# A fused block of linear attention and gated FFN: the down product as one level of Strassen, its weight combinations streamed from DRAM

## The chip, the cores and the metric

The kernel runs on one core of one Trainium2 chip. The metric is the device time of one execution in microseconds. TensorE (PE) multiplies; VectorE (DVE), ScalarE (ACT) and GpSimd (POOL) do the rest; SyncE (SP) issues nearly all DMAs. Each engine works through an order of its own and waits on semaphores.

## What is computed

u has shape (2, 2048, 512), all in float32. Cut to what matters here:

```python
xn = layernorm(u)                            # over 512
z, x, B, C, dt = split(xn @ in_proj_w)       # 1024, 1024, 64, 64, 16
x = silu(causal_conv1d(x))                   # 4 taps
y = ssd(elu(C)+1, elu(B)+1, x, decay(dt))    # 16 heads of 64, state 64
y = rmsnorm(y + D*x) * silu(z)
attn = y @ out_proj_w                        # 1024 -> 512
g = fwht(xn * SU_ug) / 64                    # Hadamard transform over 512
h = silu(g @ W_gate.T * s_g) * (g @ W_up.T * s_u)    # 2048
ffn = (fwht(h * SU_dp) / 64) @ W_down.T * s_d        # 2048 -> 512
out = u + attn + ffn
```

## The kernel before

A prologue folds the Hadamard transforms and scales into the weights and splits each weight into two float16 parts, high and low. Each product of float32 matrices is then three matmuls (high x high, high x low, low x high; `three`, line 915). All weights stay in SBUF; the down weights are `wd` (line 164), 16 chunks of 128 x 512, both parts.

Then 16 blocks of 256 rows follow (8 for each sequence, carrying a state). What each engine does in a block is written out by hand in the lists `PE_STEPS`, `ACT_STEPS`, `DVE_STEPS`, `POOL_STEPS` and `SP_STEPS` (lines 55 to 77). A name is a step with its index, and every step of a list waits for what it reads and for the buffer it writes. The steps that matter here:
- `bc`, `xp`, `z`: projections of xn from `xnT` (xn turned, in float16 parts). `elu`, `cv`, `tl`, `kl`, `dec`, `ml`, `int`, `itr`, `st`, `vl`, `sl`: the attention part. `ssq`: the root of the norm of y. `ln*`, `xh`, `xl`: layernorm and split of the next block's x.
- `F0` to `F15`: on PE, gate and up of one chunk of 128 of the 2048, 24 matmuls of 256 columns (line 936); on ACT the silu (line 1059); on DVE the product with up, into `tg` (line 1236). `H` (ACT) makes its float16 high part, `L` (DVE, line 1240) the low part, in `h`, three buffers.
- `D0` to `D15` (PE, line 943): the down product of one chunk, 2 tiles of rows x 3 matmuls of 512 columns, summed in two PSUM banks `acc`.
- `O0`, `O1` (PE, line 1003): the output product of the attention for one tile of 128 rows, added in the same banks, 24 matmuls of 512 columns each.
- `fin` (DVE, `final_sum`, line 1335): scales `acc` and adds it to the residual `res`, two operations, one block late: it stands behind `bc` of the next block.
- On SP `td` turns v, `yd` turns the gated y (two DMA transposes for each half) and `xd` turns the next x into `xnT` (four DMA transposes, `turn_x`, line 261), `res` loads the residual, `store` stores the block before. `yd11` waits for `yl11` of DVE. `xd` stands behind `yd11` in the one queue of SP, and waits itself for F15 and z11, the last readers of `xnT`. `bc` of the next block waits for all four transposes (line 923).

PSUM has 8 banks: four form a ring for all steps of `RING_READER` (line 104), each step taking the bank that the fourth step before it had; two alternate for F; two are `acc`.

The order around `bc` at a block's start is `bc xp0 xp1 F0 qk cs F1` on PE and `bc fin elu cv0 cv1 F0` on DVE.

## Time and profile before

| | |
|---|---|
| median of 3 runs | 1849.04 us (1848.91 to 1849.53) |
| profiled execution | 1849.29 us, span 1847.2 us, mean granted TensorE clock 0.996 |
| PE busy | 1794.1 us, 13746 matmuls |
| DVE busy | 1383.8 us |
| ACT busy | 1224.6 us |
| POOL busy | 307.7 us |
| DMA | 125.68 MB, mean 68 GB/s |

Line numbers (L912) are those of the kernel before; L912 is the one line that issues all matmuls of `three` and `products`. Times are in us from the start of the span. In a view in order of time the columns are start, duration, engine, line, operation, output<-input, shapes and number of instructions, and in square brackets how long the engine stood idle before it and for what. A duration reaches to the end of the last result, so it is longer than the distance to the next start. Engines that stand idle cost nothing by themselves: what counts is which wait ends last.

### The profile page before, as it was taken

The page shows a single profiled execution, that of the slowest core. Times are in us where ns is not written, and L with a number is a line of the kernel's source. Part 1 is how long each engine was busy: PE and PEld are TensorE (multiplying, and loading weights), DVE is VectorE, ACT ScalarE, POOL GpSimd, SP SyncE. Part 2 cuts the span into 40 slices and gives each one's busy share as a digit, 9 for nine tenths or more (in the row PEclk, how much of TensorE's full clock was granted, in tenths as well). Part 3 has the DMA queues.
Part 4 walks back from the last instruction along what each step waited for, and adds up shares of the span by engine and source line. Part 5 has one row for each costly group of instructions (what it writes and reads, how often), then busy time and mean ns, then how long its engine had stood idle before and what let it go on. Part 6 is the DMA issues. An engine that isn't in the chain of part 4 may idle for free.

```text
span 1847.2 us, 37874 instructions
## 1 busy us (share of the span) xinstructions
PE 1794.1 (97%) x13746; PEld 1241.8 (67%) x13746; DVE 1383.8 (75%) x2859; ACT 1224.6 (66%) x2582; POOL 307.7 (17%) x270
## 2 busy tenths in 40 slices
PE   4878999999999999999999999999999999999998
PEld 2336667576766768676766758677666757676675
DVE  6987867869586877858586877958686776958686
ACT  7967848576574848566584847666584857667483
POOL 0000212213030212203021221203021220303021
PEclk9999999999999999999999999999999999999999
DMA  8221223121312223131312322131322213131232
GB/s 326 69 69 49 56 58 81 32 82 38 81 47 62 77 47 76 41 78 41 89 47 58 81 45 76 36 77 47 86 53 58 81 34 75 43 81 47 65 75 58
DMA packets 217573, 125.68 MB, mean 68 GB/s; under 512 B 179662, under 2 KB 180790, under 8 KB 216886
## 3 DMA queue, kind: packets, MB, share of 16 engines
q1 hardware_dynamic: 216870, 122.30, 25.1%
q8 instruction: 109, 1.79, 0.4%
q10 hardware_dynamic: 528, 1.05, 0.2%
q14 instruction: 66, 0.54, 0.1%
HBM read 72.18 MB, written 8.65 MB: 44 GB/s over the span
## 4 chain that ended last, share of the span: by engine, by line
PE 90%; DVE 5%; ACT 1%; DMA 1%; issue 1%; SPq 1%; DVEq 1%; ACTq 0%
PE bank L912 88%; DVE wug L624 1%; DVE wi L666 1%; DMA wi<-n_L_attn_out_proj_w_dram 1%; PE bank L728 1%; PE bank L729 0%; DVE big L509 0%; ACT big L460 0%; DVE wo L675 0%; ACT wi L432 0%; SPq L873 0%; PE bank L717 0%; DVE wd L509 0%; DVE big L510 0%; ACT wi L464 0%
## 5 line engine op out<-in xcount | busy, mean ns | idle before, releaser
L912 PE MATMUL bank<-pair,wug 128*128 128x256 f16 x6144 | 699.8, 273 | 0.0
L912 PEld LDWEIGHTS bank<-pair,wug 128*128 128x128 f16 x6144 | 596.2, 98 | 90.4 <-issue 3.4
L912 PE MATMUL bank<-wd,h 128*128 128x512 f16 x1536 | 360.3, 379 | 0.0
L1185 POOL TENSOR_TENSOR state<-state,dec 128x512 f32<-128x512 f32 x64 | 87.5, 1377 | 1066.3 <-ACT neg L1100 805.7
L912 PEld LDWEIGHTS bank<-wd,h 128*128 128x128 f16 x1536 | 149.2, 98 | 160.4 <-DVE h L1243 0.2
L1232 DVE SCALAR_TENSOR_TENSOR pair<-pair,conv 128x256 f32<-128x256 f32 x384 | 180.2, 514 | 79.0 <-ACT pair L1048 69.1
L912 PE MATMUL bank<-wi,pair 128*128 128x512 f16 (+1 forms) x1152 | 201.6, 330 | 3.1 <-DVEq L1345 3.1
L912 PE MATMUL bank<-pair,wi 128*128 128x256 f16 x1536 | 173.1, 273 | 0.0
L912 PEld LDWEIGHTS bank<-wi,pair 128*128 128x128 f16 x1152 | 101.4, 99 | 98.1 <-issue 3.9
L1114 ACT ACTIVATE Mx<-Mx,cs_own 128x128 f32<-128x128 f32 x512 | 162.2, 388 | 7.6 <-DMA Mx<-cs_rows 7.4
L912 PEld LDWEIGHTS bank<-pair,wi 128*128 128x128 f16 x1536 | 150.0, 98 | 17.0
L1173 POOL TENSOR_TENSOR pair<-v 128x512 f32<-128x512 f16 x64 | 79.5, 1242 | 429.4 <-DMA v<-pair 381.4
L1265 DVE TENSOR_TENSOR Mx<-Mx,Gm 128x512 f32<-128x512 f32 x128 | 99.6, 778 | 32.3 <-ACT Mx L1118 22.5
L1063 ACT ACTIVATE pair<-bank,gate_scale 128x256 f32<-128x256 f32 x128 | 60.4, 472 | 92.1 <-PE bank L912 68.2
L1092 ACT ACTIVATE stateK<-state 128x512 f16<-128x512 f32 x64 | 39.7, 620 | 90.0 <-DVE state L1297 90.0
L1297 DVE SCALAR_TENSOR_TENSOR state<-bank,state 128x512 f32<-128x512 f32 x64 | 44.0, 687 | 72.6 <-PE bank L912 72.2
L1063 ACT ACTIVATE tg<-bank,gate_scale 128x256 f32<-128x256 f32 x128 | 59.9, 468 | 49.7 <-PE bank L912 48.8
L1239 DVE SCALAR_TENSOR_TENSOR tg<-tg,h_scale,bank 128x256 f32<-128x256 f32 x128 | 60.9, 476 | 37.8 <-ACT tg L1063 34.2
L1270 DVE TENSOR_TENSOR Mx<-Mx 128x512 f16<-128x512 f32 x96 | 77.2, 804 | 12.7 <-ACT Mx L1129 10.6
L1118 ACT ACTIVATE Mx<-Mx 128x512 f32<-128x512 f32 x128 | 80.6, 630 | 8.1
L912 PE MATMUL bank<-wo,yT 128*128 128x512 f16 x384 | 85.5, 379 | 0.0
L912 PE MATMUL bank<-wo,Mx 128*128 128x512 f16 x384 | 85.5, 379 | 0.0
(253 smaller groups left out, 2717.0 us busy)
## 6 DMA issues: line engine op xcount, KB each, us to landing
Mx<-cs_rows SPq DMA_DIRECT2D x128, 256.0 KB, 3.6
pair<-in_L_attn_u_dram SPq DMA_DIRECT2D x17, 512.0 KB, 3.6
Mx<-in_L_attn_u_dram SPq DMA_DIRECT2D x16, 512.0 KB, 3.7
out_dram<-Mx SPq DMA_DIRECT2D x16, 512.0 KB, 2.8
big<-in_L_ffn_W_down_dram SPq DMA_DIRECT2D x2, 2048.0 KB, 17.8
wug<-in_L_attn_in_proj_w_dram SPq DMA_DIRECT2D x2, 2048.0 KB, 13.4
pair<-in_L_ffn_W_gate_dram SPq DMA_DIRECT2D x4, 1024.0 KB, 5.3
pair<-in_L_ffn_W_up_dram SPq DMA_DIRECT2D x3, 1024.0 KB, 16.6
```

The lines of the kernel that those rows point to most:

```text
L912: ins = nc.tensor.matmul(out, lhsT, rhs, start=first and n == 0, stop=last and n == len(pairs) - 1)
L1063: nc.scalar.activation(tg[c % 2][:, :], ug[c % 2][:, 0:TB], ACT.Silu, scale=gate_scale[:, c:c + 1]).then_inc(gate_ready, 1)
L1092: nc.scalar.activation(stateK[:, hf * 512:(hf + 1) * 512], state[:, hf * 512:(hf + 1) * 512], ACT.Copy, scale=1.0 / LOW).then_inc(state_hi ...
L1114: nc.scalar.activation(M[q][:, n, :], M[q][:, n, :], ACT.Relu, scale=-1.0, bias=cs_own[:, c, 4 * q + n:4 * q + n + 1])
L1118: nc.scalar.activation(M[q][:, :, :], M[q][:, :, :], ACT.Exp, scale=-1.0).then_inc(M_exp, 1)
L1173: pool.tensor_tensor(by_tile(vd[:, :]), v16[:, 4 * hf:4 * hf + 4, c, 0, :], v16[:, 4 * hf:4 * hf + 4, c, 1, :], ALU.add)
L1185: pool.tensor_tensor(half, half, bcast(dec3[:, 2, c, 8 * hf:8 * hf + 8], HD), ALU.mult).then_inc(state_faded, 1)
L1232: ins = nc.vector.scalar_tensor_tensor(cv[n % 2][:, c, :], x[:, c, j:j + TB], conv[:, CX * j + t:CX * j + t + 1], cv[n % 2][:, c, :], ALU. ...
L1239: nc.vector.scalar_tensor_tensor(tg[c % 2][:, :], tg[c % 2][:, :], h_scale[:, c:c + 1], ug[c % 2][:, TB:2 * TB], ALU.mult, ALU.mult).then_ ...
L1265: nc.vector.tensor_tensor(M[q][:, :, :], M[q][:, :, :], Gm[:, c, :].unsqueeze(1).to_broadcast([P, 4, P]), ALU.mult).then_inc(M_whole, 1)
L1270: nc.vector.tensor_tensor(M_lo[q], M[q][:, :, :], M_hi[q], ALU.subtract).then_inc(M_ready, 1)
L1297: nc.vector.scalar_tensor_tensor(half, o[:, :], 1.0 / PEAK, half, ALU.mult, ALU.add).then_inc(dve_emptied, 1)
```

## The change

The down product of a block is a (256 x 2048) by (2048 x 512) product. The change takes it in 8 groups of 256 of the 2048 (`E0` to `E7`, two F chunks each), and each group as one level of Strassen: a matrix of 2 x 2 tiles of 128 x 128 (rows by depth) times one of 2 x 2 tiles of 128 x 256 gives seven products in place of eight. Each is three matmuls of 256 columns, summed over the groups in seven half banks of PSUM, `acc`, now four banks.
- The left sides: `S` on DVE (`half_sums`) forms five sums of the four tiles of h in three operations, with a drain ahead; `H` and `L` split seven tiles of 128 in place of two halves of 256.
- The right sides: the prologue forms five sums of each group's weight tiles on DVE (`ds`, `part_sums`, the same three operations), splits the seven on ACT (`dh`) and DVE (`dl`) in place of the 16 H steps of `wd` on DVE, and SP stores them in DRAM (`dw`). `wd` is gone. In each block ACT loads them back, 896 KB a group, into three buffers `ws` (`wl0` to `wl7`).
- `fin` adds the seven products to four quarters of `res`: six operations with drains. It moves behind `cv0`. `O0` and `O1` take a ring bank each, and DVE adds them to `res` (`out_part`), ahead of `bc` of the next block.
- F takes its bank from the ring of four, which so serves 42 steps a block; `tg` has four buffers.
- All five orders are new, those of the prologue too. The small loads of the prologue move from SP to ACT, and SP loads `nat0` and `nat1` (weights of up) first. PE starts block 0 without waiting for the whole prologue. SP's and POOL's loops over the blocks are unrolled.

The core of the diff:

```diff
 PE_STEPS = """
-bc xp0 xp1 F0 qk cs F1 xp2 xp3 F2 F3 F4 G F5 D0 D1 D2 int00 int01 F6 F7 D3 D4 D5 itr00 F8 F9 itr01 D6 st00 F10
-D7 F11 st01 D8 z00 int10 z01 D9 itr10 F12 F13 int11 D10 itr11 st10 F14 D11 z10 z11 F15 D12 O0 D13 D14 st11 D15
-O1
+bc xp0 xp1 cs xp2 qk F0 F1 F2 F3 G xp3 F4 F5 F6 int00 E0 F7 F8 E1 F9 itr00 st00 E2 int01 F10 itr01 F11 st01
+z00 F12 int10 E3 z01 E4 F13 F14 itr10 int11 st10 F15 E5 itr11 z10 z11 O0 E6 E7 st11 O1
 """.split()
 ACT_STEPS = """
-elu xp0 xb0 xp1 qk xb1 cs F0 sv0 kh sv1 th0 F1 th1 xp2 H0 H1 xp3 F2 dr00 F3 xb2 dr01 xb3 dr02 sv2 H2 th2 H3
-sv3 F4 th3 F5 de00 de01 de02 H4 H5 mh00 dr03 mh01 de03 F6 F7 mh02 H6 vh00 H7 mh03 F8 dr10 F9 de10 H8 H9 vh01
-dr11 mh10 de11 sh00 dr12 ssq0 dr13 mh11 de12 de13 F10 F11 mh12 z00 vh10 H10 H11 sh01 mh13 F12 z01 F13 yh00
-yh01 vh11 ssq1 xh0 z10 H12 H13 xh1 F14 yh10 z11 sh10 H14 yh11 F15 H15 sh11
+elu wl0 xp0 xb0 xp1 cs sv0 xb1 qk F0 th0 xp2 kh dr00 F1 sv1 th1 F2 H0 F3 xb2 dr01 xp3 xb3 wl1 sv2 dr02 th2 F4
+sv3 wl2 F5 th3 de00 H1 de01 de02 mh00 dr03 mh01 de03 F6 wl3 vh00 F7 H2 F8 mh02 H3 F9 mh03 wl4 vh01 dr10 sh00
+de10 F10 H4 ssq0 mh10 F11 dr11 z00 F12 dr12 sh01 de11 de12 vh10 wl5 dr13 de13 H5 z01 F13 mh11 mh12 F14 wl6
+yh00 mh13 wl7 yh01 vh11 F15 H6 ssq1 sh10 xh0 z10 yh10 z11 H7 yh11 xh1 sh11
 """.split()
 DVE_STEPS = """
-bc fin elu cv0 cv1 F0 kl tl0 F1 tl1 L0 L1 qk F2 F3 cv2 cv3 L2 G tl2 L3 F4 tl3 F5 dec00 dec01 dec02 L4 ml00 L5
-ml01 dec03 F6 F7 ml02 int00 L6 vl00 ml03 L7 F8 lna F9 itr00 dec10 int01 st00 L8 itr01 vl01 ml10 L9 sl00 dec11
-st01 ssq0 ml11 dec12 dec13 F10 F11 int10 ml12 L10 z00 L11 vl10 sl01 ml13 F12 itr10 lnb int11 z01 yl00 itr11
-F13 yl01 lnc vl11 ssq1 L12 z10 L13 st10 F14 yl10 z11 L14 xl0 yl11 F15 xl1 L15 st11 sl10 sl11
+O0 O1 bc elu cv0 fin cv1 qk tl0 kl F0 F1 tl1 S0 G F2 L0 F3 cv2 cv3 F4 tl2 S1 tl3 F5 dec00 L1 dec01 ml00 dec02
+S2 dec03 ml01 F6 int00 vl00 F7 L2 S3 F8 itr00 ml02 F9 ml03 st00 L3 vl01 S4 int01 dec10 F10 itr01 sl00 L4 st01
+lna F11 ssq0 z00 S5 lnb dec11 ml10 dec12 F12 vl10 dec13 int10 sl01 L5 ml11 lnc F13 F14 itr10 ml12 yl00 z01 S6
+ml13 int11 yl01 st10 itr11 vl11 L6 F15 S7 ssq1 z10 yl10 z11 xl0 sl10 yl11 L7 xl1 st11 sl11
 """.split()
 POOL_STEPS = """
-sd00 sd01 vw00 vw01 sd10 vw10 sd11 vw11
+sd00 vw00 vw01 sd01 vw10 vw11 sd10 sd11
 """.split()
 SP_STEPS = """
-store bw bd00 bd01 bd02 bd03 td0 td1 td2 td3 xin bd10 bd11 bd12 bd13 yd00 yd01 yd10 yd11 xd res
+bw bd00 store td0 bd01 td1 bd02 bd03 td2 td3 bd10 bd11 xin bd12 bd13 yd00 yd01 yd10 yd11 res xd
...
 
+            def part_sums(eng, ops, n):
+
+                b, o = part[n % 2], part_sum[n % 2]
+                eng.wait_ge(hw_high, UG_UNITS + 2 * n + 2)
+                if n >= 2:
+                    eng.wait_ge(part_ready, n - 1)
+                ops.tensor_tensor(o[:, 0:2, :], b[:, 0::2, :], b[:, 1::2, :], ALU.add)
+                ops.tensor_tensor(o[:, 2:4, :], b[:, 2:4, :], b[:, 0:2, :], ALU.subtract)
+                ops.tensor_tensor(o[:, 4, :], b[:, 0, :], b[:, 3, :], ALU.add).then_inc(part_summed, 1)
+
...
+                    elif k == "dh":
+                        act.drain()
+                        act.wait_ge(part_summed, n + 1)
+                        if n >= 2:
+                            act.wait_ge(wd_stored[n % 2], 16 * (n // 2))
+                        nc.scalar.activation(part_out[n % 2][:, 0:2, 0, :], part[n % 2][:, 0::3, :], ACT.Copy)
+                        nc.scalar.activation(part_out[n % 2][:, 2:7, 0, :], part_sum[n % 2], ACT.Copy).then_inc(part_high, 1)
...
+                    elif k == "ds":
+                        part_sums(dve, nc.vector, n)
+                    elif k == "dl":
+                        dve.wait_ge(part_high, n + 1)
+                        o = part_out[n % 2]
+                        nc.vector.tensor_tensor(o[:, 0:2, 1, :], part[n % 2][:, 0::3, :], o[:, 0:2, 0, :], ALU.subtract)
+                        nc.vector.tensor_tensor(o[:, 2:7, 1, :], part_sum[n % 2], o[:, 2:7, 0, :], ALU.subtract).then_inc(part_ready, 1)
...
             def bank(i, s):
 
                 prior, ago = before(s)
+                if kind(prior) == "F":
+                    pe.wait_ge(h_whole, (i + 1 - ago) * KF + index_of(prior) + 1)
+                    return position(s)
...
                     elif k == "F":
                         c = number(at)
-                        pe.wait_ge(h_whole, (i + 1) * KF + c - 1)
+                        o = bank(i, s)
                         for n, col in enumerate((FF + c * P, c * P)):
-                            ins = products(ug[c % 2][:, n * TB:(n + 1) * TB],
+                            ins = products(o[:, n * TB:(n + 1) * TB],
...
-                    elif k == "D":
-                        c = number(at)
-                        pe.wait_ge(h_ready, (i + 1) * KF + c + 1)
-                        if c == 0:
+                    elif k == "E":
+                        n = at[0]
+                        g = i * KG + n
+                        pe.wait_ge(h_ready, g + KG + 1)
+                        pe.wait_ge(wd_loaded[g % 3], (g // 3 + 1) * 16)
+                        if n == 0:
                             pe.wait_ge(acc_emptied, i + 1)
-                        for j in range(NT):
-                            ins = products(acc[j][:, :], three(lambda u: h[c % 3][:, u, j * P:(j + 1) * P], lambda u: wd[:, c, u, :]),
-                                           first=c == 0, last=c == KF - 1 and down_closes(j))
+                        a, w = hs[g % 2], ws[g % 3]
+                        for left, right, to in ((5, 3, M7), (2, 1, M5), (3, 0, M2), (4, 2, M6), (6, 6, M1), (1, 4, M4), (0, 5, M3)):
+                            ins = products(acc[:, to, :], three(lambda u: a[:, u, left, :], lambda u: w[:, right, u, :]),
+                                           first=n == 0 and to in (M7, M2, M1, M3), last=n == KG - 1)
                         ins.then_inc(h_used, 1)
...
-                        products(acc[c][:, :], [pq for a in range(CX) for pq in three(lambda u: yT[c][:, a, u, :], lambda u: wo[:, a, u, :])],
-                                 first=False, last=not down_closes(c)).then_inc(acc_filled, 1)
+                        o = bank(i, s)
+                        products(o[:, :], [pq for a in range(CX) for pq in three(lambda u: yT[c][:, a, u, :], lambda u: wo[:, a, u, :])]).then_inc(ring_filled, 1)
...
+                    elif k == "wl":
+                        g = i * KG + at[0]
+                        if i == 0:
...
+                        act.wait_ge(h_used, g + KG - 2)
+                        act.dma_start(ws[g % 3][:, :, :, :], wd_dram[at[0]]).then_inc(wd_loaded[g % 3], 16)
                     elif k == "H":
...
+                        n = at[0]
+                        act.wait_ge(h_used, (i + 1) * KG + n - 1)
+                        act.wait_ge(summed, (i + 1) * KG + n + 1)
+                        nc.scalar.activation(hs[n % 2][:, 0, 0:2, :], tp[n % 2][:, 0::3, :], ACT.Copy)
+                        nc.scalar.activation(hs[n % 2][:, 0, 2:7, :], hsum[:, :, :], ACT.Copy).then_inc(h_high, 1)
...
+        def half_sums(eng, ops, i, n):
+
+            x = tp[n % 2]
...
+            eng.wait_ge(h_whole, (i + 1) * KF + 2 * n + 2)
+            eng.wait_ge(h_ready, (i + 1) * KG + n)
+            ops.tensor_tensor(hsum[:, 0:2, :], x[:, 0:2, :], x[:, 2:4, :], ALU.add)
+            ops.tensor_tensor(hsum[:, 2:4, :], x[:, 1:3, :], x[:, 0::3, :], ALU.subtract)
+            ops.tensor_tensor(hsum[:, 4, :], x[:, 0, :], x[:, 3, :], ALU.add).then_inc(summed, 1)
...
+                    elif k == "S":
+                        dve.drain()
+                        half_sums(dve, nc.vector, i, at[0])
...
+                        n = at[0]
+                        dve.wait_ge(h_high, (i + 1) * KG + n + 1)
+                        nc.vector.tensor_tensor(hs[n % 2][:, 1, 0:2, :], tp[n % 2][:, 0::3, :], hs[n % 2][:, 0, 0:2, :], ALU.subtract)
+                        nc.vector.tensor_tensor(hs[n % 2][:, 1, 2:7, :], hsum[:, :, :], hs[n % 2][:, 0, 2:7, :], ALU.subtract).then_inc(h_ready, 1)
...
+            def out_part(i, j):
+                dve.wait_ge(res_loaded, i * 16)
+                dve.wait_ge(ring_filled, i * NR + filled(f"O{j}"))
+                nc.vector.scalar_tensor_tensor(res[:, j, :], position(f"O{j}")[:, :], S_OUT, res[:, j, :], ALU.mult, ALU.add).then_inc(dve_emptied, 1)
...
+                dve.wait_ge(h_used, (i + 1) * KG)
+                quarter = res[:, :, :].rearrange("p j (s n) -> p (j s) n", s=2)
+                both = lambda m: acc[:, m, :].unsqueeze(1).to_broadcast([P, 2, HALF])
+                for terms, to, scale in ((acc[:, M7:M5 + 1, :], quarter[:, 0:2, :], S_OUT), (acc[:, M2:M6 + 1, :], quarter[:, 2:4, :], S_OUT),
+                                         (both(M1), quarter[:, 0::3, :], S_OUT), (both(M3), quarter[:, 1::2, :], S_NEG),
+                                         (both(M4), quarter[:, 0::2, :], S_OUT), (acc[:, M5:M2 + 1, :], quarter[:, 0::3, :], S_NEG)):
+                    dve.drain()
+                    ins = nc.vector.scalar_tensor_tensor(to, terms, scale, to, ALU.mult, ALU.add)
+                ins.then_inc(out_ready, NT)
                 dve.wait_ge(out_ready, i * NT)
                 dve.sem_inc(acc_emptied, 1)
```

## Rows read from the trace of the kernel before

**Rows 1.** The page, part 1: busy us, share of the span.
```profile
PE 1794.1 (97%) x13746; PEld 1241.8 (67%) x13746; DVE 1383.8 (75%) x2859; ACT 1224.6 (66%) x2582; POOL 307.7 (17%) x270
```

**Rows 2.** Windows of one block: us, busy by engine, clock, DMA share, GB/s.
```profile
791.30:896.20 104.90, 104.90 (x836) 73.82 (x835) 78.25 (x162) 68.84 (x147) 18.86 (x16) 1.00 0.23 61
```

**Rows 3.** TensorE in order of time: start, us, line, operation, number.
```profile
811.86 8.02 PE L912 MATMUL bank<-pair,wug 128*128 128x256 f16 x72
819.81 0.23 PE L912 MATMUL bank<-qK,kT 64*128 64x128 f16 x1
822.88 4.05 PE L912 MATMUL bank<-wd,h 128*128 128x512 f16 x18
826.76 0.38 PE L912 MATMUL bank<-stateK,qK 128*128 128x512 f16 x1
```

**Rows 4.** VectorE in order of time, mid-block, back to back.
```profile
838.04 0.68 DVE L1279 TENSOR_TENSOR pair<-bank,dec 128x512 f32<-128x512 f32 x1
838.79 0.75 DVE L1283 SCALAR_TENSOR_TENSOR pair<-pair,scal 128x512 f32<-128x512 f32 x1
839.46 0.42 DVE L1243 TENSOR_TENSOR h<-pair,h 128x256 f16<-128x256 f32 x1
839.80 0.68 DVE L1301 TENSOR_TENSOR vw<-vw 128x512 f16<-128x512 f32 x1
840.40 0.69 DVE L1270 TENSOR_TENSOR Mx<-Mx 128x512 f16<-128x512 f32 x1
841.00 1.38 DVE L1243 TENSOR_TENSOR h<-tg,h 128x256 f16<-128x256 f32 x1
```

**Rows 5.** VectorE: first operation of bc, last of yl11.
```profile
794.44 0.48 DVE L1203 TENSOR_SCALAR raw<-bank,scal 128x256 f32<-128x256 f32 x1 [5.90 <-PE bank L912]
...
885.47 0.68 DVE L1322 TENSOR_TENSOR neg<-v,Gm 128x512 f16<-128x512 f32 x1
```

**Rows 6.** Waits of VectorE, 794.44 to 885.3: total, times, longest; first and last.
```profile
DVE raw L1203 <- PE bank L912: 5.9, 1, 5.9
...
DVE kq L1214 <- DVE Mx L1340: 0.2, 1, 0.2
```

**Rows 7.** SP's queue and TensorE ahead of a block: yd11, x, res; bc.
```profile
886.66 1.20 SPq L873 DMA_TRANSPOSE Mx<-Gm  x1
...
893.58 1.27 SPq L266 DMA_TRANSPOSE pair<-pair  x1
895.12 0.41 SPq L857 DMA_DIRECT2D Mx<-in_L_attn_u_dram  x1
...
897.63 1.66 PE L912 MATMUL bank<-wi,pair 128*128 128x144 f16 x24
```

**Rows 8.** VectorE at the start of block 0, where no fin stands.
```profile
166.82 0.43 DVE L1214 SCALAR_TENSOR_TENSOR kq<-raw,neg 128x256 f32<-128x256 f32 x1 [0.57 <-ACT neg L1053]
...
168.41 0.19 DVE L1218 SCALAR_TENSOR_TENSOR pair<-raw,pair 128x32 f32<-128x32 f32 x1 [0.96 <-ACT pair L1055]
...
170.26 2.79 DVE L1232 SCALAR_TENSOR_TENSOR pair<-pair,conv 128x256 f32<-128x256 f32 x6 [1.14 <-ACT pair L1048]
```

**Rows 9.** TensorE at the start of block 0: windows; bc in time order.
```profile
161.80:164.00 2.20, 2.13 (x19) 2.16 (x20) 1.59 (x4) 0.00 (x0) 0.00 (x0) 0.50 0.03 7
...
161.87 3.04 PE L912 MATMUL bank<-wi,pair 128*128 128x144 f16 x24 [3.08 <-DVEq L1345]
```

**Rows 10.** GpSimd in order of time.
```profile
840.65 1.45 POOL L1173 TENSOR_TENSOR pair<-v 128x512 f32<-128x512 f16 x1 [3.08 <-DVE vw L1301]
```

**Rows 11.** VectorE at the end of the last block.
```profile
1842.49 1.41 DVE L1340 SCALAR_TENSOR_TENSOR Mx<-bank,scal,Mx 128x512 f32<-128x512 f32 x2 [4.99 <-DMA Mx<-in_L_attn_u_dram]
```

**Rows 12.** DMA issues (KB each, us to landing); waits of VectorE ahead of 161.87.
```profile
pair<-in_L_attn_u_dram SPq DMA_DIRECT2D x17, 512.0 KB, 3.6
...
pair<-pair SPq DMA_TRANSPOSE x68, 2.5
...
DVE wo L509 <- DMA pair<-in_L_ffn_W_up_dram: 14.4, 2, 13.3
```

## What the change will do to the time

> **What bounds the kernel now.** I read the page's busy shares first: the matmuls are busy for 97% of the span [rows 1]. Then I cut the span into stretches. The prologue ends where bc of block 0 starts, at 161.87 us [rows 9]; 16 blocks of 104.9 us each follow. In one of them TensorE is busy for 104.90 of 104.90 us, VectorE for 78 and ScalarE for 69 [rows 2]. So a block lasts as long as its matmuls, and VectorE has 26 us left. The question is whether these 26 us are free time. The next views (VectorE in order of time, its waits, the transposes on SP's queue) say that they are not all free.
>
> **What the change gives TensorE.** Eighteen D matmuls of 512 columns take 3.88 us from start to start (822.88 to 826.76), 0.2156 each; 72 F matmuls of 256 columns take 7.95 us (811.86 to 819.81), 0.1104 each [rows 3]. A block has 16 D steps of 6 matmuls: 96 x 0.2156 = 20.70 us. It gets 8 E steps of 7 products x 3 matmuls of 256 columns: 168 x 0.1104 = 18.55 us. Each E matmul loads its own stationary, as each F matmul does, so F's price holds. The gain is 2.15 us a block, 34 us in 16, and a block can't be shorter than 102.75 us.
>
> **What it gives VectorE.** From start to start [rows 4]: a two-tensor operation of 256 elements takes 0.34 us (839.46 to 839.80), one of 512 takes 0.60 (839.80 to 840.40), so I put 640 at 0.74 and 128 at 0.21; a scalar_tensor_tensor of 512 takes 0.67 (838.79 to 839.46), so one of 256 about 0.4. A drain between two costs some 0.15 more (838.04 to 838.79 is 0.75 where 0.60 would do).
> - S, new, 8 a block: 0.34 + 0.34 + 0.21, and 0.14 for its drain. 8.2 us.
> - L: 16 x 0.34 = 5.4 us become 8 x (0.34 + 0.74) = 8.6. 3.2 us more.
> - fin: 1.41 us for two operations (the last block shows it alone [rows 11]) become six with drains, 6 x 0.81 = 4.9. 3.5 us more.
> - O0 and O1 now pass through VectorE: 2 x 0.67 = 1.3 us.
> Together 16.2 us a block, on 78 busy us plus the 5 us of small gaps that no wait accounts for: 99 of the 102.75 that TensorE would need. That alone would just fit.
>
> **Why it doesn't fit.** The next block's bc can't start before xnT is turned. SP issues these four transposes behind yd11, and yd11 waits for yl11 on VectorE. VectorE must then wait for bc before it goes on. So there is a ring: bc filled, VectorE's work up to yl11, yd11, xd, bc. Its length after the change, term by term:
> - VectorE from bc (794.44) to the end of yl11 (885.47 + 0.68 = 886.15) takes 91.7 us now [rows 5]. Twelve waits are listed in it, from 5.9 us down to 0.2 [rows 6]. The 5.9 lies ahead of the stretch, the other eleven sum to 12.0 us, most of them for something that VectorE reached early. Work: 79.7 us.
> - Added inside: S 8.2, L 7 x 1.08 - 15 x 0.34 = 2.5 (L7 comes after yl11), fin 3.5, F15 0.4 and sl10 0.7, which now stand ahead of yl11. 15.3 us.
> - Waits that stay though VectorE is late: fin no longer fills the time in which ScalarE makes exp and ln. Block 0 runs without fin and shows 0.57 and 0.96 us there, then 1.14 ahead of cv0 [rows 8]. Nothing stands between z10 and yl10 any more, so ACT's yh10 is waited for, about 0.7; S0 to L0 leaves some 0.4. 3.8 us.
> - From yl11 to xnT: yd11's first transpose is issued at 886.66, the last of x at 893.58, and it lands 2.5 us after its issue [rows 7, 12]: 9.4 us. The new SP order has res ahead of xd, 0.4 more [rows 7], and 0.1 to start. 10.0 us.
> - bc until VectorE reads it: bc takes 1.66 us [rows 7] and a semaphore's way, 1.8.
> Sum: 79.7 + 15.3 + 3.8 + 10.0 + 1.8 = 110.6 us. The same ring today has 79.7 + 9.5 + 1.8 and some 3 us of forced waits, 94: 11 us of slack, and the change adds 17. One thing lightens it: sd01 moves behind vw01 on GpSimd, so cv1 no longer runs beside two of its operations. I take 110.0 us, and TensorE idles for 7 us of it at E7, O1 and bc. As lower end I take out what meetings with GpSimd cost VectorE in the 79.7, about 3 us (four operations of that stretch are like the 1.0 us below): 107.4. As upper end I let three more us of ScalarE and DMA waits into it: 113.
>
> **GpSimd beside VectorE.** At 841.00 an L took 1.38 us where the one at 839.46 took 0.42 [rows 4], beside a GpSimd operation of 1.45 us from 840.65 [rows 10]. The 79.7 us hold such losses; the new S and L add 24 net two-tensor operations a block against the same 16 on GpSimd. The Trainium skill (SBUF — State Buffer, Who interferes with whom) says that a VectorE operation with two SBUF inputs and a GpSimd operation take a shared port in turns, the loser blocked for the whole instruction. The row agrees, and by that rule this speaks against the change: each further meeting costs up to one GpSimd operation, and one more a block makes it 111 us rather than 110.
>
> **The clock.** Block 0 starts after 3.08 us in which TensorE stood still, and the granted clock reads 0.50 there, the level of 1.2 GHz; its bc takes 3.04 us [rows 9] instead of 1.66 [rows 7]. If the wait for xnT grows as long as that, each block pays up to 1.4 us on the ring: inside my upper end. The Trainium skill (TensorE: Matmul & The Clock Gate, Part 1) has the clock halved for an idle array, which agrees.
>
> **The streamed weights.** Each wl moves 896 KB; the nearest row is 512 KB, landing 3.6 us after issue [rows 12], so 5 to 10 us. ScalarE issues each long ahead of need (wl3 behind F6, for an E3 that stands behind int10, some 25 us of matmuls on), so I count no wait for them. Price between 0 and, if they delay the v and y transposes by their own length twice a block, 3 us, which the upper end has. The issue itself costs ScalarE about 0.4 [rows 7], 8 times; it has 36 us free. H grows from 16 x 256 to 8 x 896 elements there, hidden likewise. F now shares the four ring banks; a bank is needed again three steps after it is filled, 5 to 8 us of matmuls, and VectorE, being late, reads an F in about that time: 0 to 2 us, and where it costs TensorE time the ring above hides it.
>
> **Prologue and end.** VectorE's prologue gets 8 x (0.89 + 1.08) = 15.8 us in place of 16 x 0.66 = 10.6, ScalarE 8 dh steps; against that nat0 and nat1 are loaded first, and VectorE stood 14.4 us for such loads [rows 12]. Between -10 and +8 us, I take -2. Block 8 resets the states on VectorE, which no longer hides; 1024 + 512 elements written come to some 1.7 us. The last block has no transposes of x behind it but a longer tail: yl11 ends 100 us after its bc, yd11 lands 3.9 later, O1 takes 24 x 0.2156, 5.3 with its last result, its read 0.7, fin 4.9, and the store ends the span as now, 3.3 us after VectorE (1842.49 + 1.41 to the span's end [rows 11]): 118.1 us, where it takes 110.4 now (897.63 + 8 x 104.9 to 1847.2). +7.7.
>
> **Sum**, against the profiled execution of 1849.3 us (the median is 1849.0): 15 x (110.0 - 104.9) = +76.5; +7.7; +1.7; -2. **1933 us.**
>
> **The rivals.**
> 1. *TensorE stays the bound* (the other side). It needs the ring to close in 102.75 us: VectorE's work up to yl11 would have to be under 87 us with its waits instead of 98.8. For it speaks that busy time alone fits (99 of 102.75) and that the new orders move fin behind cv0 and put sums beside it. Against it speaks the ring. It decides from some 8 us less than I count. Time: 1849.3 - 34 + 3.5 for fin at the end - 2 = 1817. Chance 0.12; a block of 104.5 to 105 and so no change: 0.04.
> 2. *The ring bites, but less*: fewer meetings with GpSimd, sums that overlap waits. Blocks of 105.5 to 107, 1860 to 1886. Chance 0.08.
> 3. *Streams and clock on top*: blocks beyond 113, over 1980. Chance 0.04.
> 4. *The ring as counted*, 107 to 113: 1886 to 1980. Chance 0.72.
> That the columns don't fall is excluded by the counts.
>
> The range reaches over 2 and nearly all of 4: **1865 to 1975**. A measurement of this kernel tells 0.2% (3.7 us) from nothing. Faster 0.12, the same 0.04, slower 0.84.
>
> **What would show it.** Right: a block of 108 to 112 us; TensorE idle for 5 to 9 us in each, ahead of E6, E7, O1 or bc, waiting for L on VectorE or for the transposes; VectorE busy for 94 us and more of a block; its wait ahead of bc still 6 to 8 us though it is the bound. The chain that ended last would run through VectorE for most of the span. Wrong: TensorE busy without a gap over a block, or a wait for ws ahead of E. My sum fails if S and L take under 1.4 us a pair, or if xnT is turned while yl11 is still open.

## The result: 2126 us, and the profile after

The changed kernel takes 2126.38 us (median of 4 runs, 2124.62 to 2131.03) against 1849.28 us for the kernel before (1848.91 to 1850.67): a ratio of 1.1501, 95% interval 1.1481 to 1.1521. The direction was forecast, the size was not: 277 us slower in place of 84.

In the names of runs below, `after` is the changed kernel, `a_...` an edit of it, `b_...` an edit of the kernel before.

The page of the changed kernel, its parts 1 and 4 (busy time and share of each engine; the chain of work that ended last):

```profile
PE 1847.7 (87%) x14898; PEld 1371.7 (65%) x14898; DVE 1715.7 (81%) x3364; ACT 1313.7 (62%) x2630; POOL 331.7 (16%) x270
...
DVE 43%; DVEq 13%; SPq 10%; PE 9%; DMA 8%; issue 8%; ACT 7%; ACTq 2%; POOL 1%; POOLq 1%
```

The windows of one block and of the 13 blocks from 2 to 14, with the columns of [rows 2]:

```profile
1033.66:1154.79 121.13, 107.68 (x906) 81.64 (x907) 97.07 (x194) 73.42 (x149) 20.12 (x16) 0.96 0.48 114
434.56:1996.54 1561.98, 1401.67 (x11779) 1064.29 (x11779) 1268.77 (x2500) 955.65 (x1937) 267.24 (x208) 0.96 0.44 115
```

The chain of the kernel before, on its page, ran through TensorE:

```profile
PE 90%; DVE 5%; ACT 1%; DMA 1%; issue 1%; SPq 1%; DVEq 1%; ACTq 0%
```

No engine is busy for the whole block any more. TensorE, 97% in [rows 1], has gaps; VectorE is busy for 1268.77 / 13 = 97.6 us of a block of 120.15; the chain runs through VectorE and its sequencer for 56%, then through SP's queue. TensorE's waits over the same 13 blocks (total us, times, longest), and then four of VectorE's:

```profile
PE bank L967 <- DVE Mx L1359: 61.8, 13, 5.0
PE bank L967 <- DVE tp L1324: 57.9, 67, 2.6
PE bank L967 <- DVE hs L1332: 23.4, 24, 1.9
```

```profile
DVE state L1386 <- PE bank L967: 33.9, 13, 2.6
DVE pair L1317 <- ACT pair L1108: 30.5, 31, 1.7
...
DVE pair L1372 <- POOL pair L1261: 16.7, 8, 6.0
DVE hsum L1228 <- issue: 13.3, 78, 0.5
```

TensorE waits some 12 us a block, nearly all of it for VectorE: once a block, for up to 5.0 us, for the low part of a decay mask (`ml11`, L1359, ahead of itr10), then for VectorE to read the shared ring's banks (L1324) and for the low parts of h (L1332). The kernel before shows no such wait in blocks 2 to 14. VectorE, although the chain runs through it, still waits in small pieces, for everybody in turn. These pieces and the time lost beside GpSimd turn out to be most of the story.

**One table for all runs.** The ring of the prediction was cut out of each trace in the same way. *Block*: from the first bc to that of block 15, divided by 15. *Stretch*: from VectorE's first operation on bc to the end of yl11, mean of blocks 2 to 15. *Work*: the time in the stretch that is covered by VectorE's instructions, gaps of under 0.15 us between instructions of one line counted in (a view in order of time merges them; without them the work is about 1 us less, with the four added operations of `b_plus16` 2.4); *idle*: the rest, other gaps of a few hundredths included. The remainder of a block (yl11, transposes, bc, VectorE) was 12.0 to 12.1 us in every run below but the kernel before and its twin with little GpSimd work, where bc stands behind TensorE's own work. Most edits spare block 0, and the *block* column has it in its mean: with small GpSimd work in an `a_` run it is some 0.8 us higher than blocks 1 to 14, so effects on the stretch are the cleaner ones. All us. Each row is one execution. The changed kernel's four executions lie within 6.4 us, 0.4 us a block; a smaller difference between two rows is no finding.

```
kernel                    span    first bc  block   stretch  work   idle
before                    1847.2  161.9     105.0    91.1    75.6   15.6
after                     2124.2  192.9     120.2   108.2    93.8   14.4
a_no_stream               2124.9  193.6     120.2   108.0    95.2   12.8
a_light_E                 2120.2  193.0     120.0   107.7    93.7   13.9
a_light_act               2110.3  193.1     119.2   107.2    93.3   13.9
a_no_sums                 2056.1  193.2     116.1   103.8    83.9   20.0
a_fin_two                 2097.5  193.4     118.7   106.3    91.0   15.4
a_small_pool              1964.7  192.9     110.3    97.4    84.6   12.9
a_small_pool_light_act    1948.6  193.4     109.3    96.4    84.3   12.1
a_small_pool_no_sums      1912.0  192.3     106.9    94.3    77.4   16.8
b_plus16                  2034.1  163.6     116.5   104.3    91.0   13.3
b_plus16_small_pool       1919.9  161.0     109.4    97.4    83.2   14.1
b_small_pool              1847.2  162.9     105.0    89.1    70.3   18.8
a_sums_on_pool            2089.3  193.6     118.0   105.8    87.3   18.5
a_pool_x_first            2084.1  189.2     117.9   105.8    87.3   18.5
a_late_waits              2127.7  194.6     120.5   108.4    92.1   16.2
a_pool_late               2155.7  193.3     122.1   110.1    86.5   23.7
a_short_prologue          2113.5  189.0     119.9   107.7    93.3   14.4
```

The prediction's sum in these terms: stretch 79.7 + 15.3 + 3.8 = 98.8. It was 108.2. Behind yl11 things came as forecast: VectorE's waits between yl11 and its first operation on bc add up to 7.3 us a block (6 to 8 forecast). TensorE's did not: 12 us in place of 5 to 9, and mostly mid-block, not at E6, E7, O1 or bc.

### The profile page after: what moved, and what is told of

Read it like the earlier page. It is cut to its first block, busy times and chain, and to the rows that moved or that the text cites. A ratio compares the mean times of both kernels' runs of the same rounds, so it can differ in the third digit from the quotient of the medians.

```text
span 2124.2 us, 40858 instructions
## 1 busy us (share of the span) xinstructions
PE 1847.7 (87%) x14898; PEld 1371.7 (65%) x14898; DVE 1715.7 (81%) x3364; ACT 1313.7 (62%) x2630; POOL 331.7 (16%) x270
## 2 busy tenths in 40 slices
DMA packets 237182, 250.74 MB, mean 118 GB/s; under 512 B 181838, under 2 KB 182966, under 8 KB 236470
## 4 chain that ended last, share of the span: by engine, by line
DVE 43%; DVEq 13%; SPq 10%; PE 9%; DMA 8%; issue 8%; ACT 7%; ACTq 2%; POOL 1%; POOLq 1%
PE bank L967 8%; SPq L920 5%; DVE pair L1317 4%; DVE Mx L1442 3%; DVE hs L1331 3%; DVE hs L1332 3%; DMA v<-pair 3%; DMA Mx<-cs_rows 2%; DVEq L1375 2%; DVEq L1326 2%; DVE Mx L1359 2%; DVE pair L236 2%; DVE Mx L1354 2%; DVE v L1377 2%; DVE v L1405 2%
## 5 line engine op out<-in xcount | busy, mean ns | idle before, releaser
L967 PE MATMUL bank<-pair,wug 128*128 128x256 f16 x6144 | 721.4, 279 | 36.2 <-DVE tp L1324 36.1
L967 PE MATMUL bank<-ws,hs 128*128 128x256 f16 x2688 | 316.3, 274 | 28.6 <-DVE hs L1332 28.6
L967 PEld LDWEIGHTS bank<-ws,hs 128*128 128x128 f16 x2688 | 261.2, 98 | 85.1 <-DVE hs L1332 40.3
L1268 POOL TENSOR_TENSOR state<-state,dec 128x512 f32<-128x512 f32 x64 | 79.2, 1247 | 808.8 <-ACT neg L1168 808.8
L1123 ACT ACTIVATE tp<-bank,gate_scale 128x256 f32<-128x256 f32 x256 | 118.8, 464 | 108.7 <-PE bank L967 57.0
L1197 ACT ACTIVATE Mx<-Mx 128x512 f16<-128x512 f32 x96 | 59.9, 624 | 164.0 <-DVE Mx L1359 164.0
L1332 DVE TENSOR_TENSOR hs<-hsum,hs 128x640 f16<-128x640 f32 x128 | 131.5, 1027 | 0.0
L1324 DVE SCALAR_TENSOR_TENSOR tp<-tp,h_scale,bank 128x256 f32<-128x256 f32 x256 | 118.6, 473 | 2.5 <-ACT tp L1123 1.0
L1331 DVE TENSOR_TENSOR hs<-tp,hs 128x256 f16<-128x256 f32 x128 | 89.3, 697 | 10.5 <-ACT hs L1137 9.3
L1359 DVE TENSOR_TENSOR Mx<-Mx 128x512 f16<-128x512 f32 x96 | 87.6, 913 | 9.9 <-ACT Mx L1197 4.9
L1261 POOL TENSOR_TENSOR pair<-pair,row 128x512 f32<-128x512 f32 x64 | 94.2, 1471 | 0.0
L1137 ACT ACTIVATE hs<-hsum 128x640 f16<-128x640 f32 x128 | 92.5, 723 | 0.0
```

The source lines that it names most:

```text
L967: ins = nc.tensor.matmul(out, lhsT, rhs, start=first and n == 0, stop=last and n == len(pairs) - 1, skip_group_check=not (first and last))
L1123: nc.scalar.activation(tg[c % 4], position(s)[:, 0:TB], ACT.Silu, scale=gate_scale[:, c:c + 1]).then_inc(gate_ready, 1)
L1137: nc.scalar.activation(hs[n % 2][:, 0, 2:7, :], hsum[:, :, :], ACT.Copy).then_inc(h_high, 1)
L1261: pool.tensor_tensor(vh, vh, bcast(row3[:, 2, 8 * hf:8 * hf + 8], HD), ALU.mult).then_inc(vd_ready, 1)
L1324: nc.vector.scalar_tensor_tensor(tg[c % 4], tg[c % 4], h_scale[:, c:c + 1], position(s)[:, TB:2 * TB], ALU.mult, ALU.mult).then_inc(h_whol ...
L1331: nc.vector.tensor_tensor(hs[n % 2][:, 1, 0:2, :], tp[n % 2][:, 0::3, :], hs[n % 2][:, 0, 0:2, :], ALU.subtract)
```

## The experiments

The theory at the start, R: a ring through VectorE sets the block, and what it lost beyond the sum is time that VectorE loses beside GpSimd. Its rivals: the streamed weights (S), and TensorE (T). Later two more, on why VectorE's idle time did not shrink.

**1. The streamed weights are free.** In `a_no_stream` only the first three pieces are loaded:

```
+                        if g < 3:
                             act.dma_start(ws[g % 3][:, :, :, :], wd_dram[at[0]]).then_inc(wd_loaded[g % 3], 16)
+                        else:
+                            act.sem_inc(wd_loaded[g % 3], 16)
```

> The changed kernel, but the weight combinations are loaded for the first three groups of block 0 only; later loads are left out (the products take stale weights), waits and orders stay. Theory R (a ring through VectorE's work up to yl11 sets the block): only the waits on late v transposes and cs rows go, about 1 us a block where GpSimd is waited for, so 118 to 119.5 us a block and 2095 to 2120 us in all. Rival S (the streamed weights explain the 10 us a block beyond the forecast): 110 us a block, 1960 us.

The block stayed at 120.2, although 115 MB of transfers are gone (the page has 136.05 MB in place of 250.74). S falls. The 1 us that R had put on late v transposes did not come either: the wait for GpSimd's product of v went (1.3 us), but VectorE's work in the stretch rose by 1.4. The Trainium skill (SBUF — State Buffer, Who interferes with whom) has a transfer never in the way of an engine's access to SBUF. This run agrees: without the transfers VectorE's work did not fall, 95.2 us for 93.8.

**2. TensorE is not the bound.** `a_light_E` makes four of the seven products:

```
-   for left, right, to in ((5, 3, M7), (2, 1, M5), (3, 0, M2), (4, 2, M6), (6, 6, M1), (1, 4, M4), (0, 5, M3)):
+   for left, right, to in ((5, 3, M7), (3, 0, M2), (6, 6, M1), (0, 5, M3)) if i else (...all seven...):
```

> The changed kernel, only that behind block 0 the Down product makes 4 of its 7 products, 72 matmuls of 128x128 less in a block, some 8 us of TensorE. (The result lacks them.) Theory R: TensorE has slack, so the block stays within 1 us of 120.2 and the span within 15 us of 2124. Rival T (TensorE is still what bounds the block, through its waits for VectorE that it can't catch up): the block falls by most of the 8 us, span about 2010 to 2040.

Its window over 13 blocks, and TensorE's longest wait there:

```profile
434.52:1992.63 1558.11, 1324.70 (x10842) 982.18 (x10842) 1268.08 (x2500) 954.38 (x1937) 268.69 (x208) 0.94 0.44 115
```

```profile
PE bank L967 <- DVE tp L1324: 109.6, 81, 4.5
```

TensorE's busy time falls by 77 us, its wait for VectorE's reading of the ring (57.9 before) rises by 52, its other waits for VectorE by 17, and the block keeps its length. T falls.

**3. GpSimd's work beside VectorE.** `a_small_pool` cuts GpSimd's four kinds of operation (three in each vw, one in each sd) from 512 columns to 32 behind block 0; VectorE's work is untouched.

```
-   pool.tensor_tensor(by_tile(vd[:, :]), v16[:, 4 * hf:4 * hf + 4, c, 0, :], v16[:, 4 * hf:4 * hf + 4, c, 1, :], ALU.add)
+   pool.tensor_tensor(vd[:, 0:32], v16[:, 4 * hf, c, 0, 0:32], v16[:, 4 * hf, c, 1, 0:32], ALU.add)
```

> The changed kernel with GpSimd's 16 operations a block cut to 32 columns behind block 0 (the rest of their work is left out). Theory R with collisions: the excess of VectorE's operations over their medians is about 10 us a block and goes almost wholly, with 1 us of waits for GpSimd: 109 to 112 us a block, 1950 to 1995 us. Rival (the excess is a slow access pattern of the new operations, not GpSimd): the 695 ns mean of L's first operation stays, and the time stays above 2100 us.

The block falls by 9.9 us, the largest effect of any single edit, the stretch, which leaves out block 0, by 10.8: work 93.8 to 84.6, with the same instructions, and 1.5 of idle time. VectorE of the changed kernel in order of time, in block 7, and GpSimd at the same time:

```profile
1117.65 1.26 DVE L1331 TENSOR_TENSOR hs<-tp,hs 128x256 f16<-128x256 f32 x1
1118.84 1.66 DVE L1332 TENSOR_TENSOR hs<-hsum,hs 128x640 f16<-128x640 f32 x1
1120.42 1.52 DVE L1359 TENSOR_TENSOR Mx<-Mx 128x512 f16<-128x512 f32 x1
1121.86 2.44 DVE L258 TENSOR_SCALAR pair<-pair 128x512 f32<-128x512 f32 x2
```

```profile
1117.07 1.56 POOL L1256 TENSOR_TENSOR pair<-v 128x512 f32<-128x512 f16 x1 [16.86 <-DVE pair L1372]
1118.77 1.04 POOL L1259 TENSOR_TENSOR vw<-pair,dec 128x512 f32<-128x512 f32 x1
1119.78 1.62 POOL L1261 TENSOR_TENSOR pair<-pair,row 128x512 f32<-128x512 f32 x1
1121.36 2.66 POOL L1268 TENSOR_TENSOR state<-state,dec 128x512 f32<-128x512 f32 x2
```

and the groups of VectorE's instructions over 13 blocks (busy us, mean ns), first of the changed kernel, then the same instructions in `a_small_pool`, where the lines are 11 further down:

```profile
L1332 DVE TENSOR_TENSOR hs<-hsum,hs 128x640 f16<-128x640 f32 x104 | 106.9, 1027 | 0.0
L1331 DVE TENSOR_TENSOR hs<-tp,hs 128x256 f16<-128x256 f32 x104 | 72.2, 695 | 9.0 <-ACT hs L1137 8.0
L1359 DVE TENSOR_TENSOR Mx<-Mx 128x512 f16<-128x512 f32 x78 | 70.9, 910 | 8.1 <-ACT Mx L1197 4.0 <-DVE v L1377 0.5
L258 DVE TENSOR_SCALAR pair<-pair 128x512 f32<-128x512 f32 x26 | 31.7, 1260 | 0.0
```

```profile
L1343 DVE TENSOR_TENSOR hs<-hsum,hs 128x640 f16<-128x640 f32 x104 | 86.2, 829 | 0.0
L1342 DVE TENSOR_TENSOR hs<-tp,hs 128x256 f16<-128x256 f32 x104 | 43.8, 422 | 7.2 <-ACT hs L1137 6.3
L1370 DVE TENSOR_TENSOR Mx<-Mx 128x512 f16<-128x512 f32 x78 | 54.4, 698 | 8.1 <-ACT Mx L1197 3.9 <-DVE v L1388 0.5
L258 DVE TENSOR_SCALAR pair<-pair 128x512 f32<-128x512 f32 x26 | 12.9, 535 | 0.0
```

Five of VectorE's instructions in a row (L258 stands for two) take two to three times their undisturbed time while five of GpSimd's run beside them (L1268 stands for two). The mean of L1331, the first operation of a low part of h, is 695 ns with GpSimd's work and 422 without, so the rival of the expectation, a slow access pattern, falls. The edit also removes the wait for GpSimd's product, 1.3 us a block. L1359 above is the ml11 for which TensorE waits longest: it ends at 1121.94, and TensorE's itr10 starts at 1122.00, after 4.94 us.

**4. The same work in the kernel before.** `b_plus16` puts four additions of 256 elements and their drains ahead of every second low part of h; `b_plus16_small_pool` cuts GpSimd's work as well, `b_small_pool` does that alone.

```
+   (four times)
+   nc.vector.tensor_tensor(low, two(ident), two(upto), ALU.add)
+   dve.drain()
```

> The kernel before, with VectorE work added that nothing uses: four operations of 256 elements with two inputs in SBUF, each with a drain, ahead of every second L, about 4 x 0.48 x 8 = 15.4 us a block. Theory R as the prediction had it (11 us of slack in the ring): a block of 104.9 + 15.4 - 11 = 109 us, and up to 4 more by meetings with GpSimd: 1915 to 1985 us. Rival O (what costs is the new orders): VectorE has 26 us free a block, so under 1870 us.

> The kernel before with the 15.4 us of VectorE work a block added (four additions of 128x256 with a drain ahead of every second low part of h), and GpSimd's products of v and of the state on 32 columns. (So its output is not the reference's.) With GpSimd's work whole the same addition gave 116.45 us a block against 104.9. If what the added work lost beyond its weight in TensorE's slack was lost to GpSimd (VectorE's excess over undisturbed durations was 6.2 us a block before), the block falls to about 109, span about 1925. If the loss is in waits alone, it stays at 114 to 116, span 2000 to 2030.

> The kernel before, with GpSimd's products of v and of the state on 32 columns in all blocks. (Its output is not the reference's.) If the time that VectorE loses beside GpSimd (7.7 us a block in the kernel with the added work) was lost in the kernel before as well and lay beside TensorE's work: VectorE's work a block falls from 78.2 to about 71 and the block stays at 104.9, span 1845 to 1850. If the loss came only with the added work, VectorE's work falls by under 3 us; a shorter block than 104.5 would show that TensorE alone did not bound the kernel before.

Windows over 13 blocks each, of the kernel before, `b_small_pool`, `b_plus16` and `b_plus16_small_pool`:

```profile
373.15:1736.81 1363.66, 1363.66 (x10844) 960.41 (x10843) 1017.15 (x2109) 894.01 (x1911) 247.19 (x208) 1.00 0.24 61
```

```profile
374.36:1738.02 1363.66, 1363.66 (x10844) 960.61 (x10843) 948.66 (x2109) 891.55 (x1911) 74.13 (x208) 1.00 0.24 61
```

```profile
397.98:1910.41 1512.43, 1392.00 (x10842) 955.27 (x10843) 1218.37 (x2525) 897.43 (x1911) 249.80 (x208) 1.00 0.22 55
```

```profile
381.78:1802.68 1420.90, 1376.28 (x10843) 954.50 (x10843) 1118.61 (x2525) 894.76 (x1911) 73.13 (x208) 1.00 0.23 59
```

In the kernel before, VectorE loses 5.3 us of each stretch to GpSimd (75.6 against 70.3), and it costs nothing: both kernels take 1363.66 us for 13 blocks, to the hundredth, because TensorE is the bound. With the additions the loss is 7.7 us (91.0 against 83.2, before rounding) and costs 7.0 of the 116.5. VectorE's work in the stretch is 15.4 us longer, 13.0 of it the additions themselves (83.2 less 70.3) and 2.4 new losses to GpSimd. So added work makes the kernel slow with no Strassen step, no stream and no new order in it: the block is 11.5 us longer, of which I had expected 4 to 8. The 11 us of slack that the prediction gave the ring were 4.

**5. Taking VectorE's work away gives only part of it back.** `a_no_sums` leaves out the sums of h behind the first piece, `a_fin_two` four of fin's six operations, `a_small_pool_no_sums` both the sums and GpSimd's columns:

```
-            ops.tensor_tensor(hsum[:, 0:2, :], x[:, 0:2, :], x[:, 2:4, :], ALU.add)
-            ops.tensor_tensor(hsum[:, 2:4, :], x[:, 1:3, :], x[:, 0::3, :], ALU.subtract)
-            ops.tensor_tensor(hsum[:, 4, :], x[:, 0, :], x[:, 3, :], ALU.add).then_inc(summed, 1)
+            eng.sem_inc(summed, 1)
```

```
+                    if i > 1 and done == 2:
+                        break
+                    done += 1
                     dve.drain()
                     ins = nc.vector.scalar_tensor_tensor(to, terms, scale, to, ALU.mult, ALU.add)
```

> The changed kernel without its three sum operations of h on VectorE (made once, then left out; the drain and all waits stay). Theory R: the ring shortens by their work, 8 x 0.9 = 7.2 us, and by the 1.8 us a block that they lose beside GpSimd: 111 us a block, 1980 us. Rival O (the new orders and the shared PSUM ring hold the block, VectorE merely follows): 117 us or more, 2070 us and over.

> The changed kernel, only that behind block 1 `fin` makes 2 of its 6 sums of the Down product's accumulators. (The rest of the result is left out.) Four sums less of some 0.87 us each, 3.5 us of VectorE a block, at a place close behind bc. Theory R: all of it is on the ring, the block falls from 120.2 to about 116.7, span about 2073. Rival W: work that lies ahead of VectorE's waits for TensorE and for the v transposes is given back as wait, the block falls by under 1.5 us, span over 2100.

> The changed kernel with two things left out behind block 0: GpSimd's products of v and of the state work on 32 columns, and the sums of h are made only for the first piece. (The output is not the reference's.) Small GpSimd work alone gave 110.3 us a block, the missing sums alone 116.1. Theory R (the ring through VectorE, and GpSimd's work beside it): without GpSimd in its way the missing sums give what they weigh, 1.04 us each, 7 of them inside the stretch from bc to the y_lo part, so the stretch falls from 97.8 to about 90.5 and the block from 110.3 to about 103, where TensorE's own 102.75 us meet it; span about 1855. Rival W (the ring is held by waits that VectorE's lighter work turns into other waits, as it did in the run without the sums): the block falls by 4 us again, to about 106, span about 1900.

Without the sums the work in the stretch falls by 9.9 us (7.2 for seven S, as the pair of runs without GpSimd's columns has it, 84.6 to 77.4; the rest are meetings with GpSimd that went with them), but the idle time rises by 5.6, and the block gains 4.2, between R's 9 and its rival's 3. The rest comes back as waits that the changed kernel hardly has. Of `a_no_sums` over 13 blocks, then the same waits in the changed kernel:

```profile
DVE Mx L1357 <- ACT Mx L1186: 23.2, 27, 0.9
DVE v L1380 <- PE bank L967: 19.3, 13, 2.3
DVE tp L1327 <- ACT tp L1123: 18.2, 36, 0.6
DVE Gm L1351 <- PE bank L967: 16.6, 13, 1.3
```

```profile
DVE Mx L1354 <- ACT Mx L1186: 4.9, 13, 0.4
DVE v L1377 <- PE bank L967: 4.6, 9, 1.0
...
DVE Gm L1348 <- PE bank L967: 1.7, 9, 0.2
DVE tp L1324 <- ACT tp L1123: 1.0, 5, 0.2
```

`fin` cut by 2.8 us gives 1.6 (1.9 in the stretch), between the two theories (3.5, and under 1.5). The two large edits nearly add up: 4.2 (sums) and 9.9 (GpSimd) alone, 13.3 together; in the stretch 4.4 and 10.8, together 13.9. With both, 106.9 us a block are left; TensorE's own 102.75 were not reached. So even without GpSimd in the way the removed sums give 3.1 of their 7.2 us in the stretch, which is rival W: work that is taken away comes back in part as waits.

**6. Is the idle time ScalarE's?** VectorE keeps 12 to 14 us idle in every stretch that is full. Theory M: the ring passes through ScalarE's work. Theory V: these are hand-over times. `a_light_act` cuts ScalarE's decay masks to 32 columns, its copy of the h sums to one of five; `a_small_pool_light_act` does the same without GpSimd's columns.

```
-   nc.scalar.activation(hs[n % 2][:, 0, 2:7, :], hsum[:, :, :], ACT.Copy).then_inc(h_high, 1)
+   nc.scalar.activation(hs[n % 2][:, 0, 2:(3 if i > 0 else 7), :], hsum[:, 0:(1 if i > 0 else 5), :], ACT.Copy).then_inc(h_high, 1)
...
-   nc.scalar.activation(M[q][:, n, :], M[q][:, n, :], ACT.Relu, scale=-1.0, bias=cs_own[:, c, 4 * q + n:4 * q + n + 1])
+   nc.scalar.activation(M[q][:, n, 0:32], M[q][:, n, 0:32], ACT.Copy)       (behind block 0)
```

> The changed kernel, only that behind block 0 ScalarE works on a quarter of the columns of the decay masks (64 instructions a block of 128x32 in place of 128x128, about 6 to 7 us less) and on one of the five h sums (about 4.5 us less), some 11 us of ScalarE less a block; VectorE's, TensorE's and GpSimd's work is as it was. (The masks and h sums are then wrong.) Theory M (the ring passes from VectorE through ScalarE and back inside the stretch, which is why VectorE keeps 14.4 us of idle time there): the idle time falls by 3 us or more, block 117 or less, span under 2080. Theory V (the idle time is made of hand-over times and of waits for the other engines' latencies, not of ScalarE's work): idle time and block change by under 1.5 us, span 2105 to 2130.

> The changed kernel with GpSimd's products on 32 columns behind block 0, as in the run with small GpSimd work alone (110.3 us a block, idle time of VectorE in the stretch 12.9), and ScalarE's masks and h sums cut as in the run before. (The output is wrong by both.) Theory M: idle time falls to 9 or 10, block about 107, span about 1915. Theory V: block 109 to 110.5, span 1945 to 1970.

The edit took 8.4 us a block off ScalarE (955.65 to 846.83 over 13 blocks; the expectation had put 11). The idle time fell by 0.5 and 0.8 us, the block by 1.0 in both. That is V's answer for the steps that were cut, the masks and the h sums. The waits for ScalarE that remain (6.0 us in the changed kernel, 4.9 here) are for steps that the edit left whole, the first tap of the convolution above all; nothing was tried on those. In the changed kernel's stretch the 14.4 us are: 4.0 in 52 gaps of under 0.12 us between instructions, 6.0 in ten waits for ScalarE, 1.4 in seven issue gaps (the first sum of each S), 1.3 for GpSimd, 1.7 others. The kernel before has 3.6, 10.8, 0.2, 0 and 0.9.

**7. Other orders.** `a_late_waits` moves two places in VectorE's list at which it stands waiting; `a_sums_on_pool` gives the sums to GpSimd; `a_pool_late` does both. All three compute everything. V and M mean something else in these two expectations: by V a wait of VectorE is as dear as its work, by M the ring changes engines inside the stretch and a moved wait comes back.

```
-O0 O1 bc elu cv0 fin cv1 qk
+O0 O1 bc elu fin cv0 cv1 qk
...
-ml01 F6 int00 vl00 F7 L2 S3 F8 itr00
+ml01 F6 F7 L2 S3 int00 vl00 F8 itr00
```

```
-sd00 vw00 vw01 sd01 vw10 vw11 sd10 sd11
+sd00 S0 S1 vw00 S2 vw01 S3 sd01 S4 vw10 S5 vw11 S6 sd10 S7 sd11
```

> The changed kernel, complete, with VectorE's order alone changed at two places where it stands waiting: `fin` goes ahead of cv0, which waits 1.1 us for ScalarE at the start of a block, and int00 with vl00 goes behind F7, L2 and S3, since its second instruction waits for GpSimd's first v product (0.93 to 1.3 us a block on average). Theory V (VectorE is full inside the ring, so its waits there are as dear as its work): the block falls by the two waits, about 2.4 us, to 117.8, span about 2088. Theory M (the ring changes engines inside the stretch, so the waits are the place where it runs through ScalarE and GpSimd, and VectorE's own removed work is given back in part, as without the sums: 4.2 of 8): the waits come back elsewhere, the block stays within 1 us of 120.2, span 2110 to 2135.

> The changed kernel, complete, only that the sums of h are made on GpSimd, spread among its work, in place of VectorE. VectorE loses 8.3 us a block, GpSimd gets at least that, and at its pace beside VectorE perhaps 12 to 20 us. Theory R with collisions as dear as seen (VectorE's instructions take twice their time or more beside GpSimd's): about as much is lost again by collisions as is saved, the block comes out between 117 and 124, span 2075 to 2185. If only VectorE's own work counted and collisions cost nothing, the block would fall to about 112, span about 2000.

> The changed kernel, complete, with the sums of h on GpSimd and the same two moves in VectorE's order (`fin` ahead of cv0, int00 and vl00 behind F7 and L2). The sums on GpSimd alone gave 117.95 us a block and 2091 us. Theory V: 2.4 us less again, block about 115.5, span about 2055. Theory M: with GpSimd later still for int00, the move of int00 gains something here (up to 1 us a block), the rest is given back: block 117 to 118, span 2075 to 2090.

The moved waits did not go away. In `a_late_waits` cv0 waits no longer, but cv1, now close behind it, waits 1.97 us in each block; and the wait for ScalarE's tp, 1.0 us in 13 blocks of the changed kernel, becomes

```profile
DVE tp L1324 <- ACT tp L1123: 24.9, 15, 4.1
```

VectorE's work fell by 1.7 us, the idle time rose by 1.8, and the block stayed within 0.3: that is M's forecast. With the sums on GpSimd VectorE has 6.5 us less work and 4.1 more idle time: 118.0. Both together are worse than either, 122.1, where I had given 115.5 or 117 to 118; neither theory has it.

**8. The prologue.** `a_short_prologue` leaves out the large sums and low parts of the down weights from the third piece on (L363, L364 and four fifths of L668); `a_pool_x_first` is `a_sums_on_pool` with one step moved on SP:

```
-dw4 dw5 dw6 xt dw7
+dw4 dw5 xt dw6 dw7
```

> The changed kernel, only that of the preparation of the down weights the large sums and low parts are left out for the pieces from the third on, some 18 us of VectorE ahead of block 0. (The weights are then incomplete.) If the 31 us by which the first bc comes later than before are VectorE's work and what hangs on it: first bc at about 175 in place of 192.9, span about 2106, the blocks unchanged. If they are DMA (the weights written to DRAM and read again, the x transposes behind them on the queue): first bc stays within 3 us of 192.9.

> The changed kernel, complete, with the sums of h on GpSimd (2091 us) and, in the preparation, the transposes of the first x ahead of the seventh write of down weights on the DMA queue, where VectorE has x ready at 181.7 us and the queue is held until 185.7. If the queue's order decides: the first bc comes about 4 us earlier (189), median about 2087, ratio to before 1.129. If what comes behind (the last weights' parts, which every engine waits for) decides: first bc within 1 us of 193, median 2091.

SP's queue and TensorE's first bc, of the changed kernel and then of `a_pool_x_first` (the views end inside bc, so they count fewer than its 24 matmuls):

```profile
156.76 28.79 SPq L399 DMA_DIRECT2D wd_rows<-mix  x7
185.68 2.04 SPq L273 DMA_TRANSPOSE pair<-pair  x1
...
192.91 1.38 PE L967 MATMUL bank<-wi,pair 128*128 128x144 f16 x10 [15.37 <-DMA pair<-pair]
```

```profile
157.16 22.50 SPq L398 DMA_DIRECT2D wd_rows<-mix  x6
180.02 1.97 SPq L272 DMA_TRANSPOSE pair<-pair  x1
...
189.19 2.08 PE L966 MATMUL bank<-wi,pair 128*128 128x144 f16 x16 [11.25 <-DVEq L1447]
```

The queue's order was worth its 4 us: the first bc came at 189.2, against 193.6 in `a_sums_on_pool`. The 13 us of VectorE work (its busy time ahead of the first bc falls from 150.4 to 137.8, not by the 18 I had put) were worth 3.9, which neither theory had: from 145 us on VectorE then waited 8.1 us for ScalarE's copies of the weights, where the changed kernel shows no such wait. `a_pool_x_first` is the fastest complete form of the change that was run: 2088.16 us (median of 4 runs, 2084.88 to 2093.57), ratio 1.1297 (1.1273 to 1.132) to the kernel before. No form of the change beat the kernel before.

## Why the prediction was right in direction and wrong in size

**Right.** TensorE ceased to be the bound, VectorE's ring took its place, and its outer legs were right: from yl11 to bc 10.2 us (10.0 counted), from bc to VectorE 1.7 (1.8 counted). The undisturbed size of the added work was right too. Without GpSimd's columns the stretch's work is 84.6 us after and 70.3 before: 14.3 where 15.3 were counted. Four of the five waits that the prediction put back came as counted: 0.51, 0.96 and 1.15 us at the block's start and 0.77 for yh10, 3.4 us together for 3.4. `a_light_E` and `a_no_stream` change nothing, as priced, and the leg of 1.7 us from bc to VectorE shows no slow bc on the ring, though the granted clock of the blocks is 0.96 and TensorE is busy for 107.8 us in a block of work that needs 102.75 by the prediction's count.

**Wrong 1, the waits that stay: 6.5 of the 9.4 us a block that the stretch is too long.** The prediction took the eleven waits inside the stretch, 12.0 us [rows 6], as "most of them for something that VectorE reached early", struck them from the stretch, and put 3.8 us of named waits back. With the small gaps, which the 79.7 us contained, that makes 7.9 us of idle time; 14.4 were there. No row of the table has less than 12.1, not even with ScalarE's work cut. The step that failed is the striking of the waits: the prediction assumed that the added work would fall where VectorE waits now. It falls where the order puts it. ScalarE's waits fell from 10.8 to 6.0 us only, and the change brought new ones: 1.2 us of issue gaps ahead of the sums, and 1.3 us for int00, whose second operation waits for GpSimd's product of v, for 6.0 us in block 8. `b_plus16` shows it without the change: 15.4 us more work, 2.2 us less idle time.

**Wrong 2, GpSimd: 3.9 us of losses, less 1.0 of work counted too high.** The prediction named the mechanism and priced one more meeting a block at 1 us, which its 110.0 left out. VectorE's loss to GpSimd in the stretch is 5.3 us before and 9.2 after (93.8 less 84.6), at 247 and 267 us of GpSimd's own work over 13 blocks. By the Trainium skill (SBUF — State Buffer, Who interferes with whom) a VectorE operation with two SBUF inputs and a GpSimd operation that reads SBUF shut each other out for whole instructions. The trace agrees, and shows the unit in which to count it: not one operation but a burst, for five of GpSimd's operations in a row meet five of VectorE's in a row. The burst above takes 6.6 us for what needs some 3.0 (422 + 829 + 698 + 2 x 535 ns). The same section counts tensor_scalar in its two-port modes among the forms that GpSimd shuts out, and L258, a tensor_scalar of 512 f32 elements with one tensor for input, agrees: it suffers most, 1260 ns against 535, though no view names the mode in which it ran.

The old loss was in the 79.7 us, as the prediction said (about 3 us, it was 5.3). What it missed is how much more work on VectorE would meet: in `b_plus16`, with the old orders, the loss rose by 2.4 us. How much of the 3.9 here comes from the new orders wasn't separated.

**Wrong 3, the prologue: +33 us.** The first bc came at 192.9 where 160 were counted. VectorE's added work there was priced as 8 x (0.89 + 1.08) us, as if each piece of weights had the size of a piece of h. It has twice that, 512 and 1280 elements in an instruction:

```profile
154.64 0.69 DVE L667 TENSOR_TENSOR mix<-mix 128x512 f16<-128x512 f32 x1
155.25 1.49 DVE L668 TENSOR_TENSOR mix<-mix 128x1280 f16<-128x1280 f32 x1
```

VectorE is busy for 150.4 us ahead of the first bc, not 132.1: 18.3 us more, where 5 were counted. And the 14.4 us of waits for loads [rows 12] that the prediction hoped to save did shrink, to 1.7, but others came in the first 60 us that the kernel before does not show:

```profile
DVE cmax L677 <- PEq L747: 11.1, 4, 5.3
DVE fsq L632 <- PE bank L737: 9.8, 1, 9.8
```

Then the queue: seven writes of weight parts stand ahead of the x transposes on SP, waiting for VectorE; one step moved there brought bc forward by 4 us in `a_pool_x_first`. What the rest of the 31 us would be without the new order of loads wasn't tried.

**Wrong 4, the end**, 127.7 us in place of 118.1: the last block has the same stretch, and the same 9.4 us are missing. The price of block 8 was short too: 123.9 us, 3.7 more than the mean, where 1.7 were counted.

Together: 15 x 10.2 = 154 for the blocks, 33 for the prologue, 9.6 for the end, less the 1.7 of block 8, which is in the blocks: 195 us, where the prediction fell short by 193. The rest is block 0 of the kernel before, 106.4 us, which the prediction's 104.9 took 1.5 too short.

**What stays open.** That the idle time is hand-over time is argued by elimination, not shown: part of ScalarE's work, part of TensorE's, the streams and two other orders were tried, and it stayed or grew. The waits for the first tap of the convolution, the largest (2.3 us a block), were not touched. Which of the remaining waits the ring runs through, and which only fill VectorE's time while another chain ends, was not shown for each. The sums' removal shortens the stretch by 4.4 us for 9.9 of work, GpSimd's by 10.8 for 9.2 of work and 1.3 of waits. So what a us on VectorE is worth seems to depend on where in the order it stands; no run tests that alone.

## What to carry to other kernels

When an engine with slack is about to become the bound, don't count its waits as room. Take its stretch on the ring, keep its idle time as it is unless you can say for each wait which added instruction will stand in it, and add the work on top: here 91.1 + 14.3 + 3.9 us of new losses is 109.3, and 108.2 was measured (the last two terms come from later runs; with the prediction's own 15.3 and 1 it is 107.4, still nearer than 98.8). Both times it came out above the measured stretch: `b_plus16` gave 104.3 where it has 106.5. Losses that the old bound hid (VectorE beside GpSimd: 5.3 us a block at no cost) come due with it, and they are cheap to measure: cut the other engine's columns in the kernel before, and read how far the busy time falls. Price a step by the shape of its tiles in the code, not by that of its namesake.

## What the runs showed of the hardware that I had not expected

- Moving the eight sums of a block, some 8 us, from VectorE to GpSimd costs GpSimd 229 us over 13 blocks (267 to 496), 17.6 a block, and frees 6.5 us of VectorE in the stretch, of which 2.3 reach the block.
- 115 MB more of DMA, 64 to 118 GB/s on average, changes the block by nothing that can be measured here.
- TensorE's busy time in a block depends on its waits: 107.8 us after against 104.9 before, though its matmuls were priced 2.15 us shorter, at a granted clock of 0.96. The clock is not all of it: `b_plus16` has the old matmuls, 9 us of waits a block and a granted clock of 1.00, and is busy for 107.1. Where TensorE isn't the bound this costs nothing; as a busy share it hides 5 of its 17 us of slack a block.
